# The softmax sums of an attention stage: a matmul in place of a transpose, and another slot for it

## The chip, the cores and the metric

The kernel runs on one core of a Trainium2 chip. The metric is the device time of one execution in microseconds (us), the median of several runs. The core has five engines that run side by side and meet at semaphores: TensorE (PE in the profile; its weight loads are listed as PEld), VectorE (DVE), ScalarE (ACT), GpSimd (POOL) and SyncE (SP), which issues most of the transfers.

## The reference

One decoder layer over `x` of 16 x 224 x 512: a Mamba block, cross-attention to a context of 750 keys with 16 heads of 32, and a feed-forward block with binarized weights. The change lies in the cross-attention:

```python
qh = split_heads(q @ Wq + bq); kh = split_heads(k @ Wk + bk); vh = split_heads(v @ Wv + bv)
logits = einsum('bhqd,bhkd->bhqk', qh, kh) / sqrt(32) + mask * -1e9
attn = softmax(logits, axis=-1)
out = einsum('bhqk,bhkd->bhqd', attn, vh)
return out @ Wo + bo          # x = x + this; q is layernorm(x), k and v are the context
```

## The kernel before

Three phases follow each other: `mamba_phase` (it also projects the keys and values, and leaves them in DRAM), `attention_phase` and `ffn_phase`. Only `attention_phase` is touched.

It works in slots. A slot is half of the keys (375 of 750) for four heads and 112 query rows. A batch item has 16 slots, so the phase has 256 of them (`N_ALL`), and about a dozen more in which the last ones drain. Each engine has a program of its own that loops over the slots and issues what is due in each. The order within an engine is fixed by that code; nothing schedules it. In what follows "slot k" is a slot's number modulo 16, and S(k) is the moment at which TensorE starts its scores.

In every slot TensorE does `scores` (L1172, four small matmuls into the four banks of `sps`), then `transpose_p` three times (L1186, four transposes each, of the exponentials of three slots ago, into a bank of `tps`). VectorE reads `sps` with the masking `tensor_tensor_reduce` (L1425, four times), makes `nmax` in odd slots (L1431), and copies the second of the three transposed tiles into `pT` (L1439). ScalarE does two exponentials (L1312) and copies the first and third tile (L1320). `scores` of a slot waits for the `tensor_tensor_reduce`s of the slot before, since `sps` has no second buffer.

Some slots carry more TensorE work behind the transposes:

- `weigh_v` (L1209), one half of attention times V for a group of four heads: slots 7, 8, 11, 12, 15, 0, 3, 4
- `project_q` (L1158), the queries of a group of heads: slots 14, 2, 5, 10, from the table `Q_AT`
- `spread_sums` (L1195): slots 9, 12, 1, 4, from `R_AT` (9, 12, 17, 20; the last two lie in the next item's slots)
- `out_proj` (L1219): slots 5 and 6, for the item before
- `transpose_h` (L1139): slot 13, for the next item

`spread_sums` turns the reciprocals of the softmax sums: VectorE takes them (`invert_sums`, L1446) and widens them to `rwide`, 112 rows by 128 columns, in slots 6, 10, 14 and 2. TensorE transposes both halves of `rwide` into one bank; in the slot after, ScalarE copies the bank to `rb` (`keep_sums`, L1326) ahead of its exponentials, and VectorE multiplies the weighted values by `rb` (`scale_o`, L1458) ahead of its `tensor_tensor_reduce`s.

The banks of `tps` are three and are handed out in turn by `take_bank`: a unit (one transposed tile, one `project_q`, one `spread_sums`, ...) takes the bank of the unit three before it and waits until that one has been read. A slot without an extra unit uses three, so each tile takes the bank that the same tile had in the slot before. After an extra unit every tile is one bank further: the first tile then waits for the copy of the second tile (VectorE's) of the slot before.

VectorE has more work in some slots: `row_stats` in slot 8 (L1472, for the item before), `stats_of_x1` in slot 10 (L1388) and `normalise` in slot 11 (L1403), for the next item. Those stand behind the `tensor_tensor_reduce`s of their slot and ahead of the copy into `pT`.

Of the kernel before, what the change touches and what calls it, by code (L numbers as in the profile page):

```python
# [997 lines left out]
def attention_phase(nc, t, x1_dram, x2_dram, k_dram, v_dram, mv_dram, mv2, row_mv, wsum, ident, shared, early, sps):  # L998
# [17 lines left out]
    TT = L // 2  # L1016
# [4 lines left out]
    GROUPS = HEADS // GROUP  # L1021
    SLOTS = HEADS
# [9 lines left out]
    pe, act, dve, pool, sp = nc.tensor, nc.scalar, nc.vector, nc.gpsimd, nc.sync  # L1032
    with ExitStack() as stack:
# [18 lines left out]
        rwide = mem.sbuf("rwide", [TT, 2, GROUP, DH])  # L1052
# [14 lines left out]
        T = 4 * P  # L1067
        LAST = (B - 1) * SLOTS
        ROWS_AT = (LAST + 13, LAST + 14, LAST + 17, LAST + 18)
        Q_AT = (-2, 2, 5, 10)  # L1070
        R_AT = (9, 12, 17, 20)
        THREE = LAST // 2 + 3
        assert THREE % 3 == 0 and (GROUP * KEYS <= 2 * F)
        tps = mem.psum("tps", [P, BANKS, BANK])
# [34 lines left out]
        def tensor_program():  # L1109
# [81 lines left out]
            def spread_sums(G):  # L1191
                bank = take_bank(("r", G, 0), "rb", G + 1)
                pe.wait_ge(S["rwide"], G + 1)
                for i in range(2):
                    mm = pe.transpose(tps[:, bank, i * TT:(i + 1) * TT], rwide[:, i].rearrange("p j d -> p (j d)"),  # L1195
                                      ident[0:TT, 0:TT])
                signal(("r", G, 0), mm)

            def weigh_v(b, g, part):
# [48 lines left out]
            for slot in slots:  # L1248
                before = 3 <= slot <= N_ALL + 2
                if slot == 3:  # L1250
                    value_bias()
                if slot == 6:
                    spread_alpha()
                if 0 <= slot < N_ALL:
                    scores(slot)
                if before:
                    for pair in range(PAIRS):
                        transpose_p(slot - 3, pair)
                for b in range(B):
                    at = slot - b * SLOTS  # L1260
                    if at in Q_AT:
                        project_q(b, Q_AT.index(at))
                    if at == -3 and b:
                        transpose_h(b, 0)
                        transpose_h(b, 1)
                    if at - SLOTS - 5 in range(2):
                        out_proj(b, at - SLOTS - 5)
                for b in range(B):
                    at = slot - b * SLOTS
                    for part in range(2):  # L1270
                        if 7 <= at - part < 7 + SLOTS and (at - part - 7) % 4 == 0:
                            weigh_v(b, (at - part - 7) // 4, part)
                    if at in R_AT:
                        spread_sums(b * GROUPS + R_AT.index(at))
                if slot in ROWS_AT:
                    transpose_rows(ROWS_AT.index(slot))
            for f in range(3):
# [3 lines left out]
        def scalar_program():  # L1281

            def keep_hT(b, part):
                act.wait_ge(S["unit"], unit_of["hT", b, part])
                act.wait_ge(S["unit"], unit_of["q", b * GROUPS - 1, 0])
                act.activation(hT[:, 2 * part:2 * part + 2, :],
                               tps[:, bank_of["hT", b, part], 0:2 * L].rearrange("p (k l) -> p k l", k=2),
                               ACT.Copy).then_inc(S["hT"], 1)

            def guess_rsqrt(b):  # L1290
                act.wait_ge(S["row_var"], b)
                act.activation(guess[:], var_eps[:], ACT.Ln).then_inc(S["row_log"], 1)
                act.wait_ge(S["row_log"], b)
                act.activation(guess[:], guess[:], ACT.Exp, scale=-0.5).then_inc(S["row_guess"], 1)

            def keep_q(G):
                g = G % GROUPS
                act.wait_ge(S["unit"], unit_of["q", G, 0])
                if G >= 2:
                    act.wait_ge(S["s_ps"], GROUP * (G - 1))  # L1300
                act.activation(q32[G % 2][:], tps[:, bank_of["q", G, 0], 0:L], ACT.Identity, bias=bq[:, g:g + 1],
                               scale=SCALE).then_inc(S["q32"], 1)

            def exponential(n):
                block, j = n // GROUP, n % GROUP
                G = block // 2
                head = G % GROUPS * GROUP + j
                act.wait_ge(S["nmax"], block + 1)
                if G >= GROUPS:
                    act.wait_ge(S["rwide"], G - GROUPS + 1)  # L1310
                scores = sc[buffer_of(block)][:, j, :]
                act.activation(scores, scores, ACT.Exp, scale=-1.0, bias=nmax[:, block % 3, j:j + 1],  # L1312
                               accum_out=esum[:, block % 2, head:head + 1]).then_inc(S["exp"], 1)

            def keep_pT(m, pair):
                tile = m * PAIRS + pair
                act.wait_ge(S["t_ps"], tile + 1)
                if m >= 2 * GROUP:
                    act.wait_ge(S["pv"], m // GROUP - 1)
                act.activation(place(m, pair), transposed(tile), ACT.Copy).then_inc(S["pt_act"], 1)  # L1320

            def keep_sums(G):
                act.wait_ge(S["unit"], unit_of["r", G, 0])
                if G:
                    act.wait_ge(S["oT"], G)
                act.activation(rb[:], tps[:, bank_of["r", G, 0], 0:L], ACT.Copy).then_inc(S["rb"], 1)  # L1326

            def sign_w1(k, loaded):
                act.wait_ge(S["w1_in"], 16 * loaded)
                act.activation(shared.s1[:, k, :], shared.raw_1[:, k, :], ACT.Sign).then_inc(S["s1"], 1)  # L1330

            def sign_w2(i):
                act.wait_ge(S["w2_in"], 16 * 4)
                act.activation(s2[i][:], raw_w2[i][:], ACT.Sign).then_inc(S["w2"], 1)

            def guess_rsqrt_x2(b):
                act.wait_ge(S["x2_var"], b + 1)
                act.activation(x2_guess[:], x2_var[:], ACT.Ln).then_inc(S["x2_log"], 1)
                act.wait_ge(S["x2_log"], b + 1)
                act.activation(x2_guess[:], x2_guess[:], ACT.Exp, scale=-0.5).then_inc(S["x2_guess"], 1)  # L1340

            def keep_rows(k):
                act.wait_ge(S["unit"], unit_of["rows", k])
                act.wait_ge(S["unit"], unit_of["q", B * GROUPS - 1, 0])
                act.activation(rowsT[0][:, k, :], tps[:, bank_of["rows", k], :], ACT.Copy).then_inc(S["rows_hi"], 1)

            for slot in slots:
                before = 3 <= slot <= N_ALL + 2
                if slot - 3 * SLOTS in range(2):
                    sign_w1(2 + slot - 3 * SLOTS, 1)  # L1350
                if slot - LAST - 14 in range(2):
                    sign_w1(slot - LAST - 14, 2)
                if slot - LAST - 10 in range(4):
                    sign_w2(slot - LAST - 10)
                ready = 2 <= slot <= N_ALL + 1
                for b in range(B):
                    at = slot - b * SLOTS
                    if at - 1 in Q_AT:
                        keep_q(b * GROUPS + Q_AT.index(at - 1))
                    if at == -2 and b:  # L1360
                        keep_hT(b, 0)
                        keep_hT(b, 1)
                    if at - 1 in R_AT:
                        keep_sums(b * GROUPS + R_AT.index(at - 1))
                if ready:
                    exponential(2 * slot - 4)
                if before:
                    keep_pT(slot - 3, 0)
                for b in range(B):
                    at = slot - b * SLOTS  # L1370
                    if at == -5 and b:
                        guess_rsqrt(b)
                    if at == SLOTS + 9:
                        guess_rsqrt_x2(b)
                if ready:
                    exponential(2 * slot - 3)
                if before:
                    keep_pT(slot - 3, 2)
                if slot in ROWS_AT:
                    keep_rows(ROWS_AT.index(slot))  # L1380
            act.preload_act_table_set("gelu_and_others")

        def vector_program(steps):
# [126 lines left out]
            for slot in slots:  # L1510
# [8 lines left out]
                    fold_bv()  # L1519
                for b in range(B):  # L1520
                    at = slot - b * SLOTS
                    if at - 1 in R_AT:
                        scale_o(b, R_AT.index(at - 1))
                if 0 <= slot < N_ALL:
                    negate_and_mask(slot)
                for b in range(B):
                    at = slot - b * SLOTS
# [491 lines left out]
```

## Time and profile before

| | us |
|---|---|
| median of 3 runs | 3479.71 (3476.09 to 3482.05) |
| the profiled execution's own time | 3482.05 |
| its span, first to last instruction | 3480.7 |
| attention phase, from the trace | about 1955 to 3039 |
| one batch item in it | 66.08 |

| engine | busy us of the span | share |
|---|---|---|
| PE | 3156.3 | 91% |
| DVE | 2647.8 | 76% |
| ACT | 2388.0 | 69% |
| POOL | 1804.3 | 52% |

The span is the time between the first and the last instruction of one profiled execution; the time of an execution has a little more around it. Busy shares are means over three phases with different limits, so a change in one phase is read from that phase's own stretch. In a timeline each row is one or several instructions of one line that follow each other; a bracket at its end gives the engine's idle time just before and what ended it.

### The profile page before, as it was taken

The page shows a single profiled execution, that of the slowest core. Times are in us where ns is not written, and L with a number is a line of the kernel's source. Part 1 is how long each engine was busy: PE and PEld are TensorE (multiplying, and loading weights), DVE is VectorE, ACT ScalarE, POOL GpSimd, SP SyncE. Part 2 cuts the span into 40 slices and gives each one's busy share as a digit, 9 for nine tenths or more (in the row PEclk, how much of TensorE's full clock was granted, in tenths as well). Part 3 has the DMA queues.
Part 4 walks back from the last instruction along what each step waited for, and adds up shares of the span by engine and source line. Part 5 has one row for each costly group of instructions (what it writes and reads, how often), then busy time and mean ns, then how long its engine had stood idle before and what let it go on. Part 6 is the DMA issues. An engine that isn't in the chain of part 4 may idle for free. (4 is left out here: it accounts for less than half of the span.)

```text
span 3480.7 us, 59577 instructions
## 1 busy us (share of the span) xinstructions
PE 3156.3 (91%) x20736; PEld 2195.8 (63%) x20736; DVE 2647.8 (76%) x4673; ACT 2388.0 (69%) x5339; POOL 1804.3 (52%) x1211
## 2 busy tenths in 40 slices
PE   5699889888899888988999799999999999999999
PEld 4566556665566556655655466666666666578887
DVE  2899999999999999999987577777777777523232
ACT  5778887778787887788875377777777777622222
POOL 2678887888787878887877000010010010055554
PEclk8899999999999999999999899999999999999999
DMA  5666765766576666766576221121121121120110
GB/s 162 159 181 188 192 166 161 200 185 166 151 200 187 166 157 184 196 168 159 164 194 186 73 69 50 53 88 47 53 84 51 50 84 66 48 73 25 34 40 24
DMA packets 286297, 425.01 MB, mean 122 GB/s; under 512 B 28753, under 2 KB 226129, under 8 KB 281394
## 3 DMA queue, kind: packets, MB, share of 16 engines
q1 hardware_dynamic: 278637, 411.44, 42.3%
q10 hardware_dynamic: 7365, 9.77, 0.9%
q8 instruction: 169, 2.77, 0.3%
q14 instruction: 126, 1.03, 0.1%
HBM read 320.12 MB, written 101.02 MB: 121 GB/s over the span
## 5 line engine op out<-in xcount | busy, mean ns | idle before, releaser
L811 POOL TENSOR_TENSOR a_hs<-a_rep,a_bmat 128x896 f32<-128x896 f32 x512 | 1060.9, 2095 | 287.8 <-PE a_yps L323 287.3
L443 ACT ACTIVATE a_states<-a_rep,a_a_neg 128x224 f32<-128x224 f32 x2048 | 793.7, 437 | 105.3 <-DVE a_hs L707 103.4
L700 DVE TENSOR_TENSOR_SCAN a_states<-a_states,a_hs 128x900 f32<-128x900 f32 x384 | 779.6, 2030 | 73.9 <-ACT a_states L443 59.6
L1425 DVE CUSTOM_DVE_ANT_0 b_sc<-sps,early_mask 112x375 f32<-112x375 f32 x1024 | 499.8, 545 | 155.5 <-PE sps L1172 150.9
L1312 ACT ACTIVATE b_sc<-b_sc,b_nmax 112x750 f32<-112x750 f32 x512 | 467.5, 913 | 8.4 <-DVE b_nmax L1431 8.4
L1186 PEld LDWEIGHTS b_tps<-ident,b_sc 112*125 112x125 f32 x3072 | 358.9, 189 | 160.6 <-issue 93.4
L345 PE MATMUL a_work<-early_scan_hT,w_in 128*128 128x224 f32 x2048 | 425.8, 363 | 9.2 <-issue 6.5
L1565 POOL TENSOR_SCALAR b_x_var<-mv 112x2 f32<-112x2 f32 x16 | 3.4, 213 | 828.0 <-DVE mv L1476 828.0
L707 DVE TENSOR_TENSOR a_hs<-a_states,a_cmat 128x896 f32<-128x896 f32 x384 | 419.2, 1092 | 13.2
L345 PEld LDWEIGHTS a_work<-early_scan_hT,w_in 128*128 128x128 f32 x2048 | 396.6, 196 | 49.4 <-issue 42.0
L1186 PE MATMUL b_tps<-ident,b_sc 112*125 112x112 f32 x3072 | 408.0, 281 | 17.0 <-DVE b_pT L1439 16.5
L1320 ACT ACTIVATE b_pT<-b_tps 125x448 f32<-125x448 f32 x512 | 275.1, 537 | 150.8 <-PE b_tps L1186 145.2
L400 PE MATMUL a_work<-ctx,a_wk 128*128 128x250 f32 x1536 | 348.6, 379 | 13.4 <-ACT kv_out L490 13.3
L404 PE MATMUL a_work<-wv,ctx 128*125 128x512 f32 x768 | 349.1, 597 | 9.4 <-ACT kv_out L487 8.9
L323 PE MATMUL a_yps<-a_hs,a_fold 128*32 128x224 f32 x4096 | 238.7, 376 | 116.1 <-POOL a_hs L818 46.0
L400 PEld LDWEIGHTS a_work<-ctx,a_wk 128*128 128x128 f32 x1536 | 289.5, 191 | 64.4 <-issue 16.4
L375 PE MATMUL a_work<-a_w_out,a_yT 128*112 128x512 f32 x512 | 251.1, 648 | 29.9 <-DVE early_du L690 29.9
L1818 ACT ACTIVATE c_g<-sps,early_b,early_alpha 128x512 f32<-128x512 f32 x112 | 87.1, 779 | 278.1 <-PE sps L1744 272.4
L1854 DVE CAST c_gT_hi<-c_g 128x512 fp32r<-128x512 f32 x112 | 66.8, 597 | 276.1 <-ACT c_g L1818 276.1
L700 DVE TENSOR_TENSOR_SCAN a_hs<-a_states,a_hs 128x900 f32<-128x900 f32 x128 | 258.9, 2022 | 23.6 <-ACT a_states L443 23.4
L323 PEld LDWEIGHTS a_yps<-a_hs,a_fold 128*32 128x32 f32 x4096 | 131.0, 114 | 225.9 <-DVE a_hs L707 104.2
L1892 POOL TENSOR_TENSOR c_gT_lo<-c_g,c_gT_hi 128x512 fp32r<-128x512 f32 x112 | 146.3, 1308 | 207.9 <-DVE c_gT_hi L1854 207.9
(199 smaller groups left out, 4967.5 us busy)
## 6 DMA issues: line engine op xcount, KB each, us to landing
a_rep<-du_scratch SPq DMA_DIRECT2D x512, 224.0 KB, 5.7
w_in<-W_in_dram SPq DMA_DIRECT2D x128, 512.0 KB, 4.4
du_scratch<-early_du SPq DMA_DIRECT2D x16, 1792.0 KB, 11.5
ctx<-ctxT_dram SPq DMA_DIRECT2D x48, 500.0 KB, 6.0
v_scratch<-kv_out SPq DMA_DIRECT2D x96, 250.0 KB
k_scratch<-kv_out SPq DMA_DIRECT2D x96, 250.0 KB, 4.7
b_keys<-k_scratch SPq DMA_DIRECT2D x8, 1500.0 KB, 9.3
b_v<-v_scratch SPq DMA_DIRECT2D x8, 1500.0 KB
```

The lines of the kernel that those rows point to most:

```text
L323: mm = pe.matmul(yps[j * DG:(j + 1) * DG, tile % 2 * L:(tile % 2 + 1) * L], fold[:], hs[(G4 * tile + j) % RING][:, q, 1:ROW], start=(q == ...
L345: mm = pe.matmul(work[:, bank, j * L:(j + 1) * L], w_in[unit % WINS][:, k, j * P:(j + 1) * P], hT[:, k, :], start=(k == 0), stop=(k == KD ...
L400: mm = pe.matmul(work[:, bank, j * WIDE:(j + 1) * WIDE], wk[:, k, (2 * half + j) * P:(2 * half + j + 1) * P], keys[:, k, :], start=(k == 0 ...
L404: mm = pe.matmul(work[0:KC, bank, :], keys[:, k, half * KC:(half + 1) * KC], wv[:, k, :], start=(k == 0), stop=(k == KD - 1))
L443: e = act.activation(rows(states[:, g % DA, :])[:, q, 1:ROW], rep[tile % REPS][:, j, 0, :], ACT.Exp, scale=a_neg[:, g % SLOTS, q:q + 1])
L700: dve.tensor_tensor_scan(state if g % G4 else whole, state, whole, 0.0, ALU.mult, ALU.add).then_inc(S["scan"], 1)
L707: dve.tensor_tensor(hh[:, :, 1:ROW], rows(states[:, g % DA, :])[:, :, 1:ROW], cmat[b % 2][:], ALU.mult).then_inc(S["hc"], 1)
L811: pool.tensor_tensor(hs[g % RING][:, :, 1:ROW], rep[tile % REPS][:, j, 1, :].unsqueeze(1).broadcast_to([P, Q, L]), bmat[b % 2][:], ALU.mul ...
L1186: mm = pe.transpose(tps[0:KC, bank, c * TT:(c + 1) * TT], sc[buffer_of(m // 2)][:, 2 * (m % 2) + head, chunk * KC:(chunk + 1) * KC], ident ...
L1312: act.activation(scores, scores, ACT.Exp, scale=-1.0, bias=nmax[:, block % 3, j:j + 1], accum_out=esum[:, block % 2, head:head + 1]).then_ ...
L1320: act.activation(place(m, pair), transposed(tile), ACT.Copy).then_inc(S["pt_act"], 1)
L1425: dve.tensor_tensor_reduce(out=sc[buffer_of(block)][:, j, cols], in0=sps[0:TT, j, 0:HALF], in1=mask[:, block % 2, cols], scale=-1.0, scala ...
```

## The change

`spread_sums` issues a plain matmul against the identity where it issued a transpose. Its slots become 8, 12, 0 and 4 (one rule in place of the table `R_AT`), and `keep_sums` and `scale_o` follow one slot later in each case, in 9, 13, 1 and 5. `project_q` moves from slot 2 to 1 and from 10 to 9; its copy on ScalarE (`keep_q`) is one slot later, as before.

```diff
-        Q_AT = (-2, 2, 5, 10)
-        R_AT = (9, 12, 17, 20)
+        Q_AT = (-2, 1, 5, 9)
...
-                    mm = pe.transpose(tps[:, bank, i * TT:(i + 1) * TT], rwide[:, i].rearrange("p j d -> p (j d)"),
-                                      ident[0:TT, 0:TT])
+                    mm = pe.matmul(tps[:, bank, i * TT:(i + 1) * TT], rwide[:, i].rearrange("p j d -> p (j d)"),
+                                   ident[0:TT, 0:TT], start=True, stop=True)
...
-                    if at in R_AT:
-                        spread_sums(b * GROUPS + R_AT.index(at))
+                    if 8 <= at < 8 + SLOTS and (at - 8) % 4 == 0:
+                        spread_sums(b * GROUPS + (at - 8) // 4)
...
-                    if at - 1 in R_AT:
-                        keep_sums(b * GROUPS + R_AT.index(at - 1))
+                    if 9 <= at < 9 + SLOTS and (at - 9) % 4 == 0:
+                        keep_sums(b * GROUPS + (at - 9) // 4)
...
-                    if at - 1 in R_AT:
-                        scale_o(b, R_AT.index(at - 1))
+                    if 9 <= at < 9 + SLOTS and (at - 9) % 4 == 0:
+                        scale_o(b, (at - 9) // 4)
```

The order on TensorE, slots 0 to 3 of the second batch item. Before (L1172 scores, L1186 transposes, L1209 `weigh_v`, L1195 `spread_sums`, L1158 `project_q`):

```order
L1172 MATMUL sps<-b_keys,b_q_0 112x375 x4
L1186 MATMUL b_tps<-ident,b_sc 125x112 x12
L1209 MATMUL b_ups<-b_pT,early_v_71 32x224 x12
L1172 MATMUL sps<-b_keys,b_q_0 112x375 x4
L1186 MATMUL b_tps<-ident,b_sc 125x112 x12
L1195 MATMUL b_tps<-ident,b_rwide 128x112 x2
L1172 MATMUL sps<-b_keys,b_q_0 112x375 x4
L1186 MATMUL b_tps<-ident,b_sc 125x112 x12
L1158 MATMUL b_tps<-early_hT,early_wq 128x224 x4
L1172 MATMUL sps<-b_keys,b_q_0 112x375 x4
```

With the change (every line number of these functions is one lower):

```order
L1171 MATMUL sps<-b_keys,b_q_0 112x375 x4
L1185 MATMUL b_tps<-ident,b_sc 125x112 x12
L1208 MATMUL b_ups<-b_pT,early_v_71 32x224 x12
L1194 MATMUL b_tps<-ident,b_rwide 128x112 x2
L1171 MATMUL sps<-b_keys,b_q_0 112x375 x4
L1185 MATMUL b_tps<-ident,b_sc 125x112 x12
L1157 MATMUL b_tps<-early_hT,early_wq 128x224 x4
L1171 MATMUL sps<-b_keys,b_q_0 112x375 x4
L1185 MATMUL b_tps<-ident,b_sc 125x112 x12
L1171 MATMUL sps<-b_keys,b_q_0 112x375 x4
```

`spread_sums` now stands behind `weigh_v` in slot 0, `project_q` in slot 1, and slot 2 has nothing but scores and transposes.

The same engine, slots 8 to 11 of that item, from the `weigh_v` of slot 8. Before:

```order
L1209 MATMUL b_ups<-b_pT,b_v 32x224 x12
L1172 MATMUL sps<-b_keys,b_q_0 112x375 x4
L1186 MATMUL b_tps<-ident,b_sc_19177 125x112 x12
L1195 MATMUL b_tps<-ident,b_rwide 128x112 x2
L1172 MATMUL sps<-b_keys,b_q_0 112x375 x4
L1186 MATMUL b_tps<-ident,b_sc_19177 125x112 x12
L1158 MATMUL b_tps<-early_hT,early_wq 128x224 x4
L1172 MATMUL sps<-b_keys,b_q_0 112x375 x4
```

With the change:

```order
L1208 MATMUL b_ups<-b_pT,b_v 32x224 x12
L1194 MATMUL b_tps<-ident,b_rwide 128x112 x2
L1171 MATMUL sps<-b_keys,b_q_0 112x375 x4
L1185 MATMUL b_tps<-ident,b_sc_19177 125x112 x12
L1157 MATMUL b_tps<-early_hT,early_wq 128x224 x4
L1171 MATMUL sps<-b_keys,b_q_0 112x375 x4
L1185 MATMUL b_tps<-ident,b_sc_19177 125x112 x12
L1171 MATMUL sps<-b_keys,b_q_0 112x375 x4
```

Slot 8 now has `weigh_v` and `spread_sums`, slot 9 `project_q`, and slot 10 neither. Slots 4 and 12 keep their places and have only the matmul in place of the transpose.

## Rows read from the trace of the kernel before

**Rows 1.** The page, part 1: busy time, share of the span, instructions.

```profile
PE 3156.3 (91%) x20736; PEld 2195.8 (63%) x20736; DVE 2647.8 (76%) x4673; ACT 2388.0 (69%) x5339; POOL 1804.3 (52%) x1211
```

**Rows 2.** One batch item by windows: length, busy of PE, PEld, DVE, ACT, POOL, clock.

```profile
2291.89:2357.97 66.08, 62.97 (x581) 41.96 (x577) 49.52 (x180) 48.96 (x111) 4.49 (x12) 1.00 0.18 62
```

**Rows 3.** Timeline of TensorE, slots 1 to 3: start, length, instructions, idle before.

```profile
2291.89 0.90 PE L1172 MATMUL sps<-b_keys,b_q 32*112 32x375 f32 x8
...
2294.97 0.90 PE L1172 MATMUL sps<-b_keys,b_q 32*112 32x375 f32 x8 [0.49 <-DVE b_half_min L1425]
...
2297.20 1.71 PE L1158 MATMUL b_tps<-early_hT,early_wq 128*128 128x224 f32 x8
2298.83 0.90 PE L1172 MATMUL sps<-b_keys,b_q 32*112 32x375 f32 x8
```

**Rows 4.** Timeline of TensorE, slot 4 and the start of slot 5.

```profile
2302.43 0.90 PE L1172 MATMUL sps<-b_keys,b_q 32*112 32x375 f32 x8
2303.26 1.56 PE L1186 MATMUL b_tps<-ident,b_sc 112*125 112x112 f32 x12
2304.75 1.34 PE L1209 MATMUL b_ups<-b_pT,early_v 125*32 125x224 f32 x24
...
2306.36 0.90 PE L1172 MATMUL sps<-b_keys,b_q 32*112 32x375 f32 x8
```

**Rows 5.** Timeline of TensorE, slots 9 to 13.

```profile
2326.58 0.90 PE L1172 MATMUL sps<-b_keys,b_q 32*112 32x375 f32 x8
...
2329.92 0.90 PE L1172 MATMUL sps<-b_keys,b_q 32*112 32x375 f32 x8 [0.58 <-DVE b_half_min L1425]
...
2333.78 0.90 PE L1172 MATMUL sps<-b_keys,b_q 32*112 32x375 f32 x8
2335.57 1.53 PE L1186 MATMUL b_tps<-ident,b_sc 112*125 112x112 f32 x12 [0.89 <-DVE b_pT L1439]
...
2338.31 0.90 PE L1172 MATMUL sps<-b_keys,b_q 32*112 32x375 f32 x8
...
2340.02 1.10 PE L1186 MATMUL b_tps<-ident,b_sc 112*125 112x112 f32 x8 [0.20 <-DVE b_pT L1439]
...
2342.66 0.90 PE L1172 MATMUL sps<-b_keys,b_q 32*112 32x375 f32 x8
...
2346.39 0.60 PE L1139 MATMUL b_tps<-ident,early_ln 112*128 112x112 f32 x4 [0.95 <-DVE b_pT L1439]
```

**Rows 6.** Timeline of VectorE: slot 1, then slots 8 to 12.

```profile
2292.86 0.55 DVE L1425 CUSTOM_DVE_ANT_0 b_sc<-sps,early_mask 112x375 f32<-112x375 f32 x1 [1.09 <-PE sps L1172]
...
2327.82 0.54 DVE L1425 CUSTOM_DVE_ANT_0 b_sc<-sps,early_mask 112x375 f32<-112x375 f32 x1
...
2330.97 0.54 DVE L1425 CUSTOM_DVE_ANT_0 b_sc<-sps,early_mask 112x375 f32<-112x375 f32 x1
...
2335.34 0.54 DVE L1425 CUSTOM_DVE_ANT_0 b_sc<-sps,early_mask 112x375 f32<-112x375 f32 x1
...
2338.34 1.00 DVE L1403 TENSOR_SCALAR early_ln<-early_xt,early_mv,early_rstd 112x512 f32<-112x512 f32 x2 [0.84 <-POOL early_rstd L128]
...
2339.79 0.54 DVE L1425 CUSTOM_DVE_ANT_0 b_sc<-sps,early_mask 112x375 f32<-112x375 f32 x1
```

**Rows 7.** Timeline of TensorE, slot 6 of the first batch item.

```profile
1982.40 1.09 PE L1228 MATMUL b_tps<-b_diag,b_ones 128*128 128x128 f32 x8
1983.43 0.90 PE L1172 MATMUL sps<-early_keys,b_q 32*112 32x375 f32 x8
```

**Rows 8.** Timeline of TensorE, slots 2 and 3 of the first item.

```profile
1963.64 1.61 PE L1172 MATMUL sps<-early_keys,b_q 32*112 32x375 f32 x8 [2.17 <-DVE b_half_min L1425]
1965.18 3.00 PE L1158 MATMUL b_tps<-early_hT,early_wq 128*128 128x224 f32 x8
1968.01 3.60 PE L1148 MATMUL b_tps<-early_wo,b_bv_wide 128*112 128x512 f32 x8
```

**Rows 9.** Timeline of TensorE, the start of slot 11 of the last item.

```profile
2995.67 0.90 PE L1172 MATMUL sps<-b_keys,b_q 32*112 32x375 f32 x8 [0.33 <-DVE b_half_min L1425]
```

## The prediction

> **What bounds the kernel now.** The page first: TensorE is busy 91% of the span, VectorE 76% [rows 1]. The change touches the attention phase alone, so I cut out one batch item of it with the windows view: 66.08 us, of which TensorE is busy 62.97, VectorE 49.52, ScalarE 48.96, at a granted clock of 1.00 [rows 2]. TensorE bounds this stretch and is idle 3.1 us of it. Every us of work added to TensorE in a slot where it does not wait is a us of the kernel; work added where it waits is free up to the wait. So I read the timeline of TensorE next, for the length of each kind of slot and for where the 3.1 us lie.
>
> A slot runs from scores to scores. With `weigh_v` alone it lasts 3.60 us (slot 3: 2298.83 to 2302.43 [rows 3, 4]), with `weigh_v` and `spread_sums` 3.93 (slot 4 [rows 4]), with `project_q` alone 3.86 (slot 2, 2294.97 to 2298.83 [rows 3]). All three are TensorE's own work. Slot 1, with `spread_sums` alone, lasts 3.08 (2291.89 to 2294.97) and contains 0.49 of waiting for VectorE [rows 3]: this is the shortest that a slot can be. VectorE starts its four reductions 0.97 after the scores start (2292.86), and the next scores follow 2.11 behind that start [rows 3, 6], together 3.08. Work of TensorE in such a light slot is partly hidden. The other waits of an item are 0.58 at the end of slot 9 (there VectorE is late by its statistics), 0.89 in slot 11 ahead of the first transposes and 0.20 in slot 12 ahead of the second, both for VectorE's copy into `pT` [rows 5]; the last, 0.95 for `transpose_h` in slot 13, is also for that copy [rows 5].
>
> **The matmul for the transpose.** The trace has no plain matmul of this shape, so I look for the nearest. `spread_sums` issues two transposes, which run as two instructions and take 0.33 to 0.34 us: slot 4 less slot 3, 3.93 - 3.60 [rows 3, 4]. A plain f32 matmul in this kernel runs as two instructions: four in the code show as x8 [rows 3, 7]. So two transposes become four matmul instructions. The nearest form is the spreading of alpha, 128x128 weights against 128 columns: eight instructions take 1.03 us up to the next scores (1982.40 to 1983.43 [rows 7]). Through both points, one more instruction costs (1.03 - 0.34) / 6 = 0.115 us, so `spread_sums` costs 2 x 0.115 = 0.23 us more. Bounds: above, the `project_q` matmuls with 224 columns, 1.63 us for eight (2297.20 to 2298.83 [rows 3]), 0.20 each, 0.41 more; below, `weigh_v`, 24 instructions with 32 columns of weights that overlap each other, 1.28 in slot 4 (3.60 - 0.83 for scores - 1.49 for twelve transposes [rows 4]), 0.05 each, 0.11 more; not below nothing, because the weights are as wide as before and there are twice as many instructions. I take 0.23, since rows 7 differ from the new form only in 128 columns for 112.
>
> The Trainium skill, "TensorE: Matmul & The Clock Gate", Back-to-back issue gap, gives N/2.4 + 2.5 ns for an isolated full-clock matmul, 49 ns at 112 columns. An estimate by it is 0.10 us more per `spread_sums`, and the whole sum below would come to about 3489. Rows 7 speak against it: at 128 columns the formula says 56 ns, and the row gives 115, at f32 and with a weight load ahead of each.
>
> **Slots 0 to 2.** Before: slot 0 with `weigh_v` 3.60, slot 1 with `spread_sums` 3.08, slot 2 with `project_q` 3.86: 10.53 by unrounded starts. After: slot 0 has both, 3.93 + 0.23 = 4.16; slot 1 `project_q`, 3.86; slot 2 is empty, and its floor is the 3.08 of VectorE. Sum 11.10, that is 0.57 more: 0.23 for the matmuls, 0.34 because `spread_sums` lay in a slot that had room and now lies in a full one, while the room has moved to slot 2, where nothing uses it. `scale_o` in slot 1 in place of 2 costs nothing: with it, in slot 10 now, VectorE starts its reductions 1.05 after the scores (2330.97 against 2329.92 [rows 5, 6]), and 1.05 + 2.11 = 3.16 is covered by a slot of 3.86; without that cover it would cost 0.08. `keep_sums` stands ahead of ScalarE's exponentials, and ScalarE has 17 us idle an item [rows 2].
>
> **Slot 4.** Full before and after: 0.23 more.
>
> **Slots 8 to 12.** Here a wait goes and another comes, so I follow them on the clock of rows 5, from S(8) = 2326.58 - 3.60 = 2322.98.
> - S(9) = 2322.98 + 4.16 = 2327.14 (was 2326.58).
> - The extra unit in slot 8 makes the first transposes of slot 9 wait for VectorE's copy of slot 8, done at 2327.82 [rows 6] and seen 0.23 later (as 2335.34 and 2335.57 stand to each other [rows 5, 6]), at 2328.05; they would start at 2327.14 + 0.83 = 2327.97. Wait 0.08. Slot 9 lasts 3.86 + 0.08: S(10) = 2331.08 (was 2329.92).
> - Slot 10 is empty: S(11) = 2331.08 + 3.08 = 2334.16 (was 2333.78). VectorE starts its reductions at 2331.08 + 0.97 = 2332.05; from there through the reciprocals, `stats_of_x1` and the copy it takes 4.37 (2330.97 to 2335.34 [rows 6]), so the copy is done at 2336.42 and seen at 2336.65.
> - In slot 11 no extra unit came before, so it is the second transposes that wait for it, not the first: they could start at 2334.16 + 0.83 + 0.50 (a third of 1.49) = 2335.49 and wait 1.16. Before, from the first transposes to S(12) it took 2.74 (2335.57 to 2338.31 [rows 5]); from the second it is 2.24. S(12) = 2338.89 (was 2338.31).
> - In slot 11 VectorE goes through reductions, `nmax`, `normalise` and copy. That took 4.45 with 0.84 of waiting for GpSimd's rstd in it (2335.34 to 2339.79 [rows 6]). The rstd waited for ScalarE's guess, which stands behind the copy of the first transposed tile of slot 11; that tile comes 0.6 earlier now while VectorE comes 1.1 later, so the 0.84 goes: 3.61. Copy done at 2340.03, seen at 2340.26; the second transposes of slot 12 could start at 2338.89 + 1.33 = 2340.22. The wait in slot 12 is down to 0.04; before it was 2340.02 - (2338.31 + 1.33) = 0.38 [rows 5].
> - S(13) = 2338.89 + 4.16 + 0.04 = 2343.09, was 2342.66: 0.43 more. The two matmul terms are 0.46 of it, so the moves come out even here.
>
> The SP queue is not moved in any of this, and no transfer waits for the moved steps: loads of x1, keys and values hang on `row_stats`, scores and `weigh_v`.
>
> **The sum.** 0.57 + 0.23 + 0.43 = 1.23 us an item; slots 8 to 12 occur in this form in the first 15 items, slots 0 to 2 and 4 behind 15 items: 18.5 us. Two ends differ.
> - The first item starts at the lower clock: the eight instructions of `project_q` last 3.00 there and 1.71 later [rows 3, 8]. TensorE waited 2.17 for VectorE at the end of slot 1, up to 1963.64, and `project_q` in slot 2 took 2.83 (1965.18 to 1968.01) with nothing to wait for [rows 8]. Moved into slot 1 it fills the wait and sticks out 0.6 or 0.7; slot 2 is shorter by 2.83. Gain 2.2.
> - In the last item slot 10 waits 0.33 for VectorE at its end although it has `project_q` [rows 9], so taking that away gives little back. Of slots 8 and 9, longer by 0.56 and 0.60, I keep 1.1; `spread_sums` in slots 12 and 0 is hidden, and the very last costs 0.2.
> Total 18.5 - 2.2 + 1.1 + 0.2 = 17.6 us. The profiled execution took 3482.05 (span 3480.7 and 1.35 around it), so it would take 3499.6. It was the slowest of three; on the median, 3479.7, the forecast is 3497.3.
>
> **Rivals.**
> 1. The four matmul instructions are cheap (0.11 per `spread_sums`, the lower bound): 15 x 4 x 0.12 = 7 us less, 3490, or 3487 if 0.2 an item of the waits goes my way too. For it: narrow matmuls elsewhere. Against it: rows 7.
> 2. They are dear (0.41): 15 x 4 x 0.18 = 11 us more, 3508. For it: `project_q` at 0.20 each. Against: that has twice the columns.
> 3. The waits of slots 11 to 13 dissolve, and the kernel gets faster. The place is VectorE's copy of slot 10: if the empty slot 10 lets VectorE catch up, the 1.16 that I charge in slot 11 and the wait of 0.95 for `transpose_h` [rows 5] go: 1.23 - 1.16 - 0.95 = -0.88 an item, 13 less in 15 and 1 less at the ends, 3466. It takes effect once the copy of slot 10 is done before 2335.49 - 0.23 = 2335.26, and my line puts it at 2336.42. Against it: those 4.37 of VectorE stand in slot 10 whatever TensorE does.
> 4. The added work is hidden by waits I do not see moving, and the sum is near nothing: 3480. For it: 3.1 us idle an item. Against: slots 0, 4, 8 and 12 are full in the rows.
>
> **How the numbers follow.** Forecast 0.60, rival 1 0.14, rival 2 0.07, rival 3 0.09, rival 4 0.10. A difference under 0.2% (7 us) can't be told from none here. Slower: the forecast, rival 2 and two thirds of rival 1, 0.76. Within 0.2%: the rest of rival 1 and rival 4, 0.15. Faster: 0.09. The time is 3497. The range is 3485 to 3507: the lower end takes in rival 1, the upper nearly rival 2; rivals 3 and 4 are left out.
>
> **What the profile after would show.** L1194 x4 per `spread_sums` (256 in all, not 128), 0.57 from its start to the next scores (0.34 + 0.23). A batch item of 67.3 in place of 66.08. Slots 2 and 10 at 3.08 with a wait of 0.8 for VectorE at their end; the wait in slot 11 for `pT` now inside the transposes and about 1.1; none to speak of in slot 12. The start of the first item 2.2 shorter. The prediction is wrong if an item lasts under 66.5, if `spread_sums` takes under 0.45, or if slot 2 or 10 lasts other than 3.1.

## The result and the profile after

| | before | after |
|---|---|---|
| median | 3478.12 (3476.09 to 3482.05, 4 runs) | 3510.3 (3506.99 to 3520.05, 4 runs) |
| ratio, 95% interval | | 1.0097 [1.0082, 1.0112] |
| attention phase, from the first scores to the first matmul of the phase behind it | 1083.1 | 1113.7 |
| a regular batch item | 66.08 | 67.49 |

The change makes the kernel about 1% slower: 32 us between the medians. Between the two profiled executions it is 33.6 us of span (3480.7 and 3514.3), of which 30.6 lie in the attention phase. The rest lies in the phases ahead of and behind it, which the change does not touch; over the fourteen traces of this document the attention phase starts anywhere from 1950.3 to 1960.4 us. So the readings below go by the phase, and not by single times. The direction is as predicted; the time, 3497 forecast and 3507 at most, is not.

First the page's line of busy times, as in [rows 1]:

```profile
PE 3186.9 (91%) x20864; PEld 2223.5 (63%) x20864; DVE 2650.7 (75%) x4673; ACT 2396.1 (68%) x5339; POOL 1805.3 (51%) x1211
```

TensorE is busy 30.6 us more. The added instructions are in that number (1.23 us in a regular item), but so is every us in which the same instruction ran at half the clock. The page cannot tell them apart: its row of clocks rounds each 88 us slice to a tenth. The windows view of the kernel after can (columns as in [rows 2]; the third number from the end is the granted clock). First one batch item, then slots 10, 11 and 12 of another item, then the stretch of lower clock in its slot 11, and slot 11 of the last item:

```profile
2297.11:2364.60 67.49, 64.20 (x588) 43.25 (x584) 49.63 (x181) 49.55 (x111) 4.52 (x12) 1.00 0.18 60
2135.34:2138.41 3.07, 2.39 (x21) 1.70 (x21) 2.08 (x9) 2.87 (x7) 0.00 (x0) 1.00 0.86 341
2138.41:2144.82 6.41, 5.43 (x45) 3.25 (x45) 5.83 (x19) 4.55 (x11) 1.95 (x6) 0.73 0.32 103
2144.82:2149.04 4.22, 4.22 (x53) 2.87 (x49) 2.50 (x9) 1.88 (x4) 1.54 (x2) 1.00 0.33 125
2141.22:2144.63 3.41, 3.41 (x32) 2.11 (x30) 3.06 (x11) 2.15 (x5) 1.44 (x5) 0.50 0.33 113
3028.65:3035.30 6.65, 6.65 (x44) 4.05 (x44) 5.30 (x17) 3.58 (x9) 0.00 (x0) 0.50 0.24 3
```

The first row is the item that the prediction worked out: 67.31 predicted, 67.49 measured, clock 1.00 throughout. The third row is what it did not have: slot 11 with a mean granted clock of 0.73, 6.41 us in place of 4.80. For 3.41 us of it the clock is 0.50, the level of 1.2 GHz, while TensorE is 100% busy. TensorE's timeline of the same place (columns as in [rows 3]) shows what came before:

```profile
2136.16 1.56 PE L1185 MATMUL b_tps<-ident,b_sc 112*125 112x112 f32 x12
2138.41 0.90 PE L1171 MATMUL sps<-early_keys,b_q 32*112 32x375 f32 x8 [0.68 <-DVE b_half_min L1424]
2139.24 0.69 PE L1185 MATMUL b_tps<-ident,b_sc 112*125 112x112 f32 x4
2140.91 1.70 PE L1185 MATMUL b_tps<-ident,b_sc 112*125 112x112 f32 x8 [0.98 <-DVE b_pT L1438]
2142.53 2.35 PE L1208 MATMUL b_ups<-b_pT,early_v 125*32 125x224 f32 x24
2144.82 0.90 PE L1171 MATMUL sps<-early_keys,b_q 32*112 32x375 f32 x8
...
3028.65 1.61 PE L1171 MATMUL sps<-b_keys,b_q 32*112 32x375 f32 x8 [2.29 <-DVE b_half_min L1424]
3030.19 2.86 PE L1185 MATMUL b_tps<-ident,b_sc 112*125 112x112 f32 x12
3032.98 2.47 PE L1208 MATMUL b_ups<-b_pT,b_v 125*32 125x224 f32 x24
```

TensorE waits 0.68 at the end of the empty slot 10 and 0.98 in slot 11, with 1.5 us of work between. Right behind the second wait eight transposes take 1.70, not 1.10, and `weigh_v` 2.35, not 1.34. This happens in 6 of the first 15 items (2, 6, 8, 10, 12 and 14, counted from 0), at 1.6 us each. In the last item it happens behind a wait of 2.29. Now slots 10 to 12 of an item where the clock held, with the two waits of the same length, which answers to [rows 5]:

```profile
2340.80 0.90 PE L1171 MATMUL sps<-b_keys,b_q 32*112 32x375 f32 x8
2341.63 1.56 PE L1185 MATMUL b_tps<-ident,b_sc 112*125 112x112 f32 x12
2343.87 0.90 PE L1171 MATMUL sps<-b_keys,b_q 32*112 32x375 f32 x8 [0.69 <-DVE b_half_min L1424]
2344.70 0.69 PE L1185 MATMUL b_tps<-ident,b_sc 112*125 112x112 f32 x4
2346.37 1.10 PE L1185 MATMUL b_tps<-ident,b_sc 112*125 112x112 f32 x8 [0.98 <-DVE b_pT L1438]
2347.40 1.34 PE L1208 MATMUL b_ups<-b_pT,b_v 125*32 125x224 f32 x24
2348.67 0.90 PE L1171 MATMUL sps<-b_keys,b_q 32*112 32x375 f32 x8
...
2352.26 0.70 PE L1194 MATMUL b_tps<-ident,b_rwide 112*128 112x112 f32 x4
2352.89 0.58 PE L1171 MATMUL sps<-b_keys,b_q 32*112 32x375 f32 x4
```

Slot 11 lasts 4.80 here. The last rows give the cost of `spread_sums`: 2352.26 to 2352.89, 0.63 up to the next scores. The group of its line (count, then shortest, median and longest instruction) has the doubled number:

```profile
L1194 PE MATMUL b_tps<-ident,b_rwide x256: 275/275/363, 1995.9 to 3065.3; 112*128 112x112 f32 x128
```

### The profile page after: what moved, and what is told of

Its sections match the earlier page's. It is cut to its first block and busy times, and to the rows that moved or that the text cites. A ratio compares the mean times of both kernels' runs of the same rounds, so it can differ in the third digit from the quotient of the medians.

```text
span 3514.3 us, 59833 instructions
## 1 busy us (share of the span) xinstructions
PE 3186.9 (91%) x20864; PEld 2223.5 (63%) x20864; DVE 2650.7 (75%) x4673; ACT 2396.1 (68%) x5339; POOL 1805.3 (51%) x1211
## 3 DMA queue, kind: packets, MB, share of 16 engines
q8 instruction: 170, 2.79, 0.3%
```

## The experiments

After the result I held this theory: the added matmuls and the full slots cost about 1.4 an item, and the rest is TensorE's clock, which falls because the moves put two waits close together. The rivals: the clock falls because of the plain matmuls, because of the transfers that run in slots 10 and 11, or by chance. "Falls" below counts the items among the first 15 whose slot 11 has the lower clock. The attention phase is measured in each kernel's profiled execution. Before has 1083.1 and no falls, after 1113.7 and 6. The count leaves out the first item's slot 5 and the last item, which come up behind the experiments.

**e1: the matmul alone**, in the old slots.

```diff
-                    mm = pe.transpose(tps[...], rwide[...], ident[0:TT, 0:TT])
+                    mm = pe.matmul(tps[...], rwide[...], ident[0:TT, 0:TT], start=True, stop=True)
```

> The kernel before, with the plain matmul in spread_sums and nothing moved. Theory (the added time is the matmul where TensorE is full, the moves, and a fall of TensorE's clock in slot 11 that the two waits of slots 10 and 11 bring): the matmul takes 0.63 in place of 0.34; slots 4 and 12 are full and last 4.22 in place of 3.93, slots 1 and 9 hide it and stay at 3.08 and 3.34. 0.58 an item, about 3487 against 3478, slot 11 at 4.5 in every item. Rival (the matmul form itself brings the lower clock): slot 11 or others at lower clock in about half of the items, 3495 or more. Rival (it costs in full everywhere): 1.16 an item, 3496.

Measured: 1.0014 [1.0005, 1.0024], attention 1088.3, a regular item 66.64, no falls. Slots 4 and 12 are longer by 0.29, slots 1 and 9 unchanged, since they have room. The matmul by itself costs 0.56 an item, and no slot 11 has the lower clock. The Trainium skill, "Perfetto Trace Analysis", Transposes, tells to make transposes with the transpose operation and not with a standard matmul; this run is that rule's price here.

**e2: the moves alone**, `spread_sums` still a transpose.

```diff
-        Q_AT = (-2, 2, 5, 10); R_AT = (9, 12, 17, 20)
+        Q_AT = (-2, 1, 5, 9);  (spread_sums in slots 8, 12, 0, 4, as in the change)
```

> The changed kernel with the transpose back in spread_sums, all moves kept. Theory: slots 0 to 2 last 3.93 + 3.86 + 3.08, 0.34 more than before; slots 8 to 12 about 0.2 more; slot 11 still waits 0.98 behind the 0.68 of slot 10, and lasts 6.4 in place of 4.8 at lower clock in about half of the items: 8 for the moves, 10 for the clock, 4 back at the start, some 3 in the last item, 3495 against 3478. Rival (the matmul brings the lower clock): slot 11 at 4.8 in every item, 3485.

Measured: 1.0058 [1.0041, 1.0074], attention 1099.6, a regular item 66.61, and 5 falls (items 10 to 14). The falls need no plain matmul. TensorE's timeline in an item of e2 without a fall, slots 10 and 11:

```profile
2326.48 1.56 PE L1185 MATMUL b_tps<-ident,b_sc 112*125 112x112 f32 x12
2328.72 0.90 PE L1171 MATMUL sps<-b_keys,b_q 32*112 32x375 f32 x8 [0.68 <-DVE b_half_min L1424]
2329.55 0.69 PE L1185 MATMUL b_tps<-ident,b_sc 112*125 112x112 f32 x4
2331.21 1.10 PE L1185 MATMUL b_tps<-ident,b_sc 112*125 112x112 f32 x8 [0.97 <-DVE b_pT L1438]
```

It is the same pair of waits, 0.68 and 0.97. Of the two parts of the edit only the moves make it.

**e3: the change, with the wait of slot 10 filled.** The third tile of slot 10 is transposed twice over, useless work in a slot that waits anyway.

```diff
-                for c in range(4):
+                twice = pair == 2 and (m + 3) % SLOTS == 10
+                for c in [*range(4)] * (1 + twice):
```

> The changed kernel with more work: in slot 10 TensorE does the last four transposes twice, which fills 0.5 of the 0.68 that it waits there for VectorE. Theory (the clock falls because TensorE waits 0.68 and 0.98 within 2.6 us): slot 10 stays at 3.08 with a wait of about 0.2, and slot 11 lasts 4.8 in every item: some 8 less than the changed kernel, 3501. Rival (the fall has another cause: the transfers of keys that run in slots 10 and 11, or chance): slot 11 at 6.4 in about half of the items, 3510. Rival (the empty slot is short of time): the added 0.5 is paid in each item, 3518.

Measured: 1.0058 [1.0043, 1.0073], attention 1105.5, a regular item 67.48, one fall. Its timeline, slots 10 and 11:

```profile
2332.82 2.00 PE L1186 MATMUL b_tps<-ident,b_sc 112*125 112x112 f32 x16
2335.06 0.90 PE L1171 MATMUL sps<-b_keys,b_q 32*112 32x375 f32 x8 [0.25 <-DVE b_half_min L1425]
2335.89 0.69 PE L1186 MATMUL b_tps<-ident,b_sc 112*125 112x112 f32 x4
2337.55 1.10 PE L1186 MATMUL b_tps<-ident,b_sc 112*125 112x112 f32 x8 [0.97 <-DVE b_pT L1439]
```

Sixteen transposes instead of twelve, the wait down from 0.68 to 0.25, the item as long as before the filling, and falls down from 6 to 1. The transfers are those of the change, so they alone do not bring the falls. A kernel got faster by added work: 1.0058 of the time of before and not 1.0097, with intervals that do not meet.

**e4: the matmul and the moves of slots 0 to 2 alone**; slots 8 to 12 as in before but for the matmul.

```diff
-        Q_AT = (-2, 2, 5, 10); R_AT = (9, 12, 17, 20)
+        Q_AT = (-2, 1, 5, 10); R_AT = (9, 12, 16, 20)
```

> The matmul, and of the moves only those of slots 0 to 2 (spread_sums in 9, 12, 0, 4, project_q in 14, 1, 5, 10). Theory: slots 0 to 2 last 11.16 (0.63 more than before), slots 4 and 12 0.29 more each, slot 9 hides its matmul: 1.21 an item, 4 less at the start, no item with slot 11 above 4.6: about 3492. Rival (the lower clock comes from the light slot 2 as well): slots at lower clock near slot 3 in about half of the items, 3500 or more.

Measured: 1.0056 [1.0041, 1.0072]; a regular item 67.27, no falls, attention 1097.7. The item, the clock and the phase (14.6 over before, 14 expected) are as expected; the time, 3499.7, is 7 to 8 above the 3492. Part of that is the reference: before has 3480.3 beside it and not 3478. In the trace 18.2 us of span come on top of before's, 14.6 in the attention phase, 2.5 ahead of it and 1.3 behind it, where nothing was changed. Why those two differ stays open.

**e5: before, with VectorE's copy earlier.** Both waits, that ahead of slot 11 and that within it, end on VectorE. Here its copy into `pT` moves ahead of the row statistics, the normalisation and the reciprocals of its slot. Neither the matmul nor the moves are in it.

```diff
                 negate_and_mask(slot)
+                if before:
+                    keep_pT(slot - 3)
                 ... (stats_of_x1, normalise, invert_sums, row_stats)
-                if before:
-                    keep_pT(slot - 3)
```

> The kernel before with one change on VectorE: its copy into pT stands right behind the reductions and nmax of its slot, ahead of invert_sums, row_stats, stats_of_x1 and normalise. Theory (TensorE's waits in slots 11 and 12 are for that copy, and only because the statistics stand ahead of it): slot 11 falls from 4.53 to about 3.7 (then bound by the reductions, which start as late as before), slot 12 from 4.35 to 3.9; slot 9 stays at 3.34 and slot 13 at 4.26. 1.3 an item, 19 in all, about 3461 against 3480. Rival (VectorE's total work in slots 10 to 12 is what binds): the waits move to the scores, no change, 3480.

Measured: 0.9939 [0.9925, 0.9953], faster than before; attention 1061.0, a regular item 64.79, no falls. The windows row of one item, with the clock at 1.00:

```profile
2281.99:2346.78 64.79, 62.60 (x580) 41.84 (x576) 49.39 (x181) 49.05 (x111) 4.50 (x12) 1.00 0.19 63
```

TensorE's timeline in it, slot 11 and the start of slot 12:

```profile
2327.47 0.90 PE L1172 MATMUL sps<-b_keys,b_q 32*112 32x375 f32 x8
2328.30 1.56 PE L1186 MATMUL b_tps<-ident,b_sc 112*125 112x112 f32 x12
2329.79 1.34 PE L1209 MATMUL b_ups<-b_pT,b_v 125*32 125x224 f32 x24
2331.13 0.90 PE L1172 MATMUL sps<-b_keys,b_q 32*112 32x375 f32 x8
```

VectorE's timeline behind the masking of slot 10:

```profile
2326.54 0.62 DVE L1439 COPY b_pT<-b_tps 125x448 f32<-125x448 f32 x1
...
2327.58 1.28 DVE L1388 BATCH_NORM_STATS2 early_stats<-early_xt 112x6 f32<-112x512 f32 x2
```

The copy stands ahead of the 1.28 us of statistics, so slot 11 starts its transposes 0.83 behind its scores with no wait: 3.66 in place of 4.53. This is the 0.89 of [rows 5], which the change pushed around and did not remove.

**e6: the change, with the same early copy.**

> The changed kernel with the same early copy. The wait of 0.98 inside slot 11 goes, one of about 0.7 for the reductions stands at the end of slot 11 in its place: slot 11 4.4 in place of 4.8, item 67.1. Theory (the clock falls from waits that lie close together): the waits of 0.68 and 0.7 now lie 4.4 apart in place of 2.6, so few or no items at lower clock; 0.4 x 15 + 8 less than the changed kernel, 3496. Rival (the light slot 10 alone brings it): still 5 or 6 items with slot 11 about 1.6 longer, 3505.

Measured: 1.0039 [1.0026, 1.0052], attention 1099.0, a regular item 67.05, no falls. The profiled execution is the slowest of eight (3501.7, the median is 3491.1), and its last item has the lower clock. TensorE's timeline, slots 10 and 11:

```profile
2340.14 0.90 PE L1171 MATMUL sps<-b_keys,b_q 32*112 32x375 f32 x8 [0.68 <-DVE b_half_min L1424]
2340.97 1.56 PE L1185 MATMUL b_tps<-ident,b_sc 112*125 112x112 f32 x12
2342.46 1.34 PE L1208 MATMUL b_ups<-b_pT,b_v 125*32 125x224 f32 x24
2344.50 0.90 PE L1171 MATMUL sps<-b_keys,b_q 32*112 32x375 f32 x8 [0.70 <-DVE b_half_min L1424]
```

There are still two waits, 0.68 and 0.70, but with 3.7 us of work between them in place of 1.5. The falls are gone, and that with slot 10 as light as in the change. The change keeps its other costs: against e5 it is 2.3 an item longer.

**e7 and e8: the change, with the wait of slot 11 filled**, and with both filled.

```diff
+                twice = pair == 0 and (m + 3) % SLOTS == 11                      (e7)
+                twice = (pair, (m + 3) % SLOTS) in ((2, 10), (0, 11))            (e8)
```

> The changed kernel; in slot 11 TensorE does the first four transposes twice, which fills half of the wait of 0.98 there (slot 10 keeps its 0.68). Theory (both waits together bring the lower clock, and filling either helps): slot 11 stays at 4.8 and at most 2 items of 15 show 6.4. Rival (only the wait of slot 10 matters): 5 or 6 items at 6.4. Rival (chance or transfers): the same 5 or 6.

> The changed kernel with both fills, 0.5 us of repeated transposes in slot 10 and in slot 11. Theory: item 67.49 in every item, none at the lower clock (item 3 aside, which ScalarE holds up with its signs of w1), although TensorE does 1 us more an item. Rival (transposes do not keep the clock up, only plain matmuls do; the one item of 15 with the first fill was luck): 5 or 6 items at 6.4.

Measured, one run each: e7 3502.1, attention 1105.6, waits 0.68 and 0.54; e8 3497.5, attention 1101.8, waits 0.25 and 0.54. No falls in either. Single times say little here, as the start of the phase moves by up to 10 us; the items do not, and they are in the table below.

**e9 and e10: the change and e7 again**, unaltered, for the counts.

> The changed kernel again, for another count of items whose slot 11 is at the lower clock. Theory (its two waits bring the lower clock): 3 to 8 of 15 items with slot 11 about 1.6 longer. Rival (the 6 of the first trace were that execution's chance, and e7 and e8 show the usual): 0 or 1.

> The kernel of e7 again (half of the wait in slot 11 filled). Theory: 0 to 2 items of 15 at the lower clock in slot 11. Rival (chance): as many as the changed kernel, 3 to 8.

Measured: e9 3510.3, attention 1117.0, six falls again, though in other items (1, 3, 5, 7, 9, 13); e10 3504.2, 1106.8, none. In item 1 of e9 the clock stays low into slot 12:

```profile
2061.88 0.90 PE L1171 MATMUL sps<-b_keys,b_q 32*112 32x375 f32 x8 [0.68 <-DVE b_half_min L1424]
...
2064.37 1.99 PE L1185 MATMUL b_tps<-ident,b_sc 112*125 112x112 f32 x8 [0.98 <-DVE b_pT L1438]
2066.29 2.47 PE L1208 MATMUL b_ups<-b_pT,b_v 125*32 125x224 f32 x24
2068.69 1.61 PE L1171 MATMUL sps<-b_keys,b_q 32*112 32x375 f32 x8
2070.23 1.87 PE L1185 MATMUL b_tps<-ident,b_sc 112*125 112x112 f32 x12
```

So the number of falls repeats, and which items have them does not. In both executions the lower clock begins close to the end of the second wait, from 0.3 us ahead of it to 0.4 behind. It lasts 3.41 us, in two items of e9 (1 and 9) 6.83. The falls of one execution are not independent of each other: after has them in every second item from 6 to 14, e2 in five items in a row. So 6 of 15 is less evidence than fifteen separate tries would be, and the executions have to be compared as wholes.

**e11: as e3, the filling made of plain matmuls.** The third tile of slot 10 is made by matmuls against the identity; `out` and `tile_in` are what the transpose writes and reads.

```diff
+                    if pair == 2 and (m + 3) % SLOTS == 10:
+                        mm = pe.matmul(out, tile_in, ident[0:TT, 0:TT], start=True, stop=True)
```

> The changed kernel with the third tile of slot 10 made by plain matmuls against the identity in place of transposes: about the same 0.5 us more of TensorE in slot 10 as the first fill, done by matmuls. Theory (it is the waiting that counts, not the kind of instruction): as with the first fill, 0 to 2 items of 15 at the lower clock. Rival (transposes hardly count as work, matmuls do): 0 here as well, so only 3 or more items here would speak against both; with 0 the two stay apart by e3 alone. Slot 10 stays at 3.1; the four matmuls take 8 instructions at 0.12 to 0.14.

Measured: 3503.7, attention 1104.4, waits 0.24 and 0.98, one fall, as in e3. The Trainium skill, "TensorE: Matmul & The Clock Gate", Part 4, says of the full clock that it "doesn't engage" for transposes and that they don't count as busy in the same way. By that rule e11 would have kept the clock and e3 not. They came out alike, one fall each, though in one trace each. And the full clock does reach transposes here: twelve of them take 1.56 where the granted clock is 1.00 and 2.86 where it is 0.50. The traces do not agree with the rule.

**e12: e5, and in the first item alone `project_q` in slot 1 in place of 2**, the one move that the prediction had as a gain.

```diff
-        Q_AT = (-2, 2, 5, 10)
+        Q_OF = [(-2, 1, 5, 10)] + [(-2, 2, 5, 10)] * (B - 1)
```

> The kernel of e5 (copy into pT early) with one of the moves of the change kept: project_q in slot 1 in place of 2, in the first item alone, where TensorE waits 2.2 for VectorE at the end of slot 1. Theory (this is the one place where a move pays): slots 0 to 2 of the first item 2.5 shorter, about 3455.5 against 3458 for e5; too little to tell by the times, told by the trace. Rival (the clock, low at that point, stays low longer): no gain.

Measured: 0.993 [0.9914, 0.9947], 3456.1 against 3458.2 of e5, which these intervals do not tell apart. In the trace the first item is 1.4 shorter (61.25 against 62.63), not the 2.5 expected: TensorE stays at the lower clock longer.

All of it side by side, the waits in the order in which they come. The last column, from the first scores of item 1 to those of item 15, leaves out the two ends of the phase, which differ between executions for reasons of their own:

| kernel | waits around slots 10 and 11 | falls in 15 | attention us | items 1 to 14, us |
|---|---|---|---|---|
| after, e9 | 0.68, then 0.98 | 6, 6 | 1113.7, 1117.0 | 956.1, 959.0 |
| e2 | 0.68, 0.97 | 5 | 1099.6 | 942.5 |
| e3, e11 | 0.25, 0.97 | 1, 1 | 1105.5, 1104.4 | 948.0, 948.1 |
| e7, e10 | 0.68, 0.54 | 0, 0 | 1105.6, 1106.8 | 946.4, 946.4 |
| e8 | 0.25, 0.54 | 0 | 1101.8 | 946.4 |
| e6 | 0.68, 0.70 but 3.7 of work between | 0 | 1099.0 | 940.1 |
| before | 0.58 (slot 9), 0.89 but 4.8 of work between | 0 | 1083.1 | 928.2 |
| e1, e4 | 0.32 (slot 9), 0.89 but 4.8 of work between | 0, 0 | 1088.3, 1097.7 | 934.9, 943.5 |
| e5, e12 | 0.75 (slot 9), none in slot 11 | 0, 0 | 1061.0, 1058.5 | 909.9, 908.8 |

Three traces with both waits as in the change have 6, 6 and 5 falls; six with one of them shortened, or with more work between, have 1, 1, 0, 0, 0 and 0.

Two places speak for caution. In the first item TensorE waits 0.68 at the end of slot 3 and 1.64 at the end of slot 4, with 2.4 of work between. In after and in e2, e3 and e6 to e11 slot 5 then has the lower clock for a part and lasts 6.4; in before, e1, e4, e5 and e12 it lasts 4.8, with the same two waits. Here are the rows of after, then one of before, where `project_q` takes 1.71 in place of 2.79:

```profile
1979.19 0.90 PE L1171 MATMUL sps<-early_keys,b_q 32*112 32x375 f32 x8 [1.64 <-DVE b_half_min L1424]
1980.02 2.17 PE L1185 MATMUL b_tps<-ident,b_sc 112*125 112x112 f32 x12
1981.99 2.79 PE L1157 MATMUL b_tps<-early_hT,early_wq 128*128 128x224 f32 x8
...
1980.86 1.71 PE L1158 MATMUL b_tps<-early_hT,early_wq 128*128 128x224 f32 x8
```

So a pair of waits is what the falls follow, but it does not decide alone. And in the last item slot 11 is at the lower clock, in whole or in part, in all kernels with the change's slots 8 to 12 but e8; neither the filling of one wait nor the early copy prevents it there.

## Why the prediction was wrong

The direction and the steps within an item were right. Start to start, predicted and then measured:

- Slots 0 to 2: 11.10 and 11.16. Slot 2 lasts 3.07, as its floor said.
- Slot 8: 4.16 and 4.22. Slot 9: 3.94 and 3.87; the small wait of 0.08 isn't there. Slot 10: 3.08 and 3.07.
- Slot 11: 4.73 and 4.80 where the clock holds, with a wait of 1.16 predicted inside the transposes and 0.98 measured. Slot 12: 4.20 and 4.22, without a wait.
- An item: 67.31 and 67.49.

**The step that failed is the sum.** It took every duration at the granted clock of 1.00 that [rows 2] showed, and had no term for the clock. The prediction computed that slot 10 would wait some 0.8 and slot 11 1.16 behind it, wrote both down as lengths of slots, and did not ask what two waits in a row do to TensorE. The trace of before held the warning, in the fourth batch item, of which the prediction uses no row. There TensorE waits 1.50 for ScalarE, and the transposes behind it take 2.67 in place of 1.56:

```profile
2160.83 0.41 PE L1195 MATMUL b_tps<-ident,b_rwide 112*128 112x112 f32 x2 [1.50 <-ACT b_pT L1320]
2161.17 0.90 PE L1172 MATMUL sps<-b_keys,b_q 32*112 32x375 f32 x8
2162.00 2.67 PE L1186 MATMUL b_tps<-ident,b_sc 112*125 112x112 f32 x12
2164.46 2.28 PE L1158 MATMUL b_tps<-early_hT,early_wq 128*128 128x224 f32 x8
```

This too is one that comes and goes: in e1 the same wait of 1.50 is followed by transposes at 1.56.

The 30.6 us of the attention phase, by what they are:

| term | predicted | measured |
|---|---|---|
| items 1 to 14 without 3, at full clock | 13 x 1.23 = 16.0 | 13 x 1.41 = 18.3 |
| six items with the lower clock in slot 11 | 0 | 9.7 |
| first item | 0.43 - 2.2 = -1.8 | -3.75 + 1.61 + 0.80 = -1.3 |
| item 3 | 1.2 | 0.0 |
| last item and drain | 0.57 + 0.23 + 1.3 = 2.1 | 4.0 |
| sum | 17.6 | 30.6 |

In all, the lower clock cost 9.7 in the six items, 2.0 in the last and 1.6 in the first; it gave back 1.6 in item 3 and 1.2 at the start of the phase, both because before had it there.

- **The matmul was mis-sized, but little.** `spread_sums` takes 0.63 and not 0.57: 0.29 more than the transposes, not 0.23. Four times 0.06 is 0.24 an item, of which slot 9 gives 0.06 back. That is 2.3 us of the 13 missing.
- **The last item.** That slot 10 "gives little back" was right: it lasts 4.67, and 4.68 before. But the wait in it is 2.29 now, not 0.33 [rows 9], because `project_q` no longer covers it, and slot 11 behind it runs at the lower clock: 6.73 us in place of 4.74. It is the same missing term once more.
- **Item 3** gained what the others lost: before, the lower clock stands in its slot 2 (5.50 us in place of 3.86); after, it has none, and that pays for the longer slots (68.87 us before, 68.85 after).
- **The first item** came out near the prediction by luck; three parts of it differ. Slots 0 to 2 are 3.75 shorter (15.46 and 11.70), not 2.2. The move gave some 2.6 of that, as e4 shows (12.90), where the lower clock lasts through slots 0 and 1, as it does in before. Its wait of 2.17 stayed (2.18), since the next scores still wait for VectorE, but `project_q` no longer costs a slot of its own. The other 1.2 is the clock, which in after's execution was at 1.00 for the first 3.4 us of the phase. Slot 5 lost 1.61 to the lower clock, a term that the prediction did not have. Slots 8 to 12 lost 0.80, not 0.43.
- **Rival 2** (3508) came nearest by luck: the matmuls are not dear, at 0.29 more and not 0.41. Rival 3 asked the right question about VectorE's copy of slot 10. The moves do not bring it forward; e5, which does, is the faster kernel.

Shown by the runs: the falls come with the moves (e2) and not with the matmul (e1); shortening either wait (e3, e7, e8, e11) or putting work between them (e6) takes nearly all of them away from items 0 to 14, while the full-clock item stays the same in four of these five. That the kind of filling does not matter rests on one trace each. Left open: which items fall, since it differs between executions of one program; why the first item's slot 5 falls in nine traces and not in five; why plain matmuls cost 0.06 more than the interpolation said; and what makes the untouched phases of e4 longer.

Of the two changes made together, the costs are more than the sum. The matmul adds 0.56 an item and the moves 0.53, together 1.41: in e1 two of the four matmuls hide in slots 1 and 9, and the moves take exactly that room away. In return the longer slot 8 covers a wait of 0.23 for VectorE's copy, which e2 has in slot 9.

## What to carry to other kernels

When an edit creates or lengthens a wait on TensorE, price the work behind the wait at both clock levels, and look for every other wait near it; here the fixed sum at the clock of before was only the lower end. Look in the old trace for a single stretch that already has such a wait, since it shows the price. When a light slot waits for another engine, shorten what that engine does ahead of what is waited for: reordering VectorE's copy won 0.6%, where moving TensorE's work between slots lost 0.6% (e2), a part of it to the lower clock.

## What the runs showed of the hardware

- Two waits of 0.68 and 0.98 us, neither long by itself, with 1.5 of work between, were followed by a granted clock of 0.50 for 3.41 us (twice 6.83) in some items and not in others of the same program: 6 of 15 in each of two executions.
- Full and half clock come and go behind the same waits: 0.68 and 1.64 in the first item were followed by the lower clock in nine traces of fourteen, a single wait of 1.50 in before but not in e1.
- Useless transposes kept the clock up as well as useless matmuls: one fall in 15 each.
- A plain f32 matmul of 112 columns runs as two instructions. Four instructions, with 112x128 weights, take 0.63 us up to the next work; eight, with 112x125 weights in e11, take 1.04 with the last one's tail:

```profile
2335.76 1.04 PE L1188 MATMUL b_tps<-ident,b_sc 112*125 112x112 f32 x8
```

  Transposes of the second size run as one instruction each, twelve in 1.49 up to the next work.
